# Causal mask by VectorE in the row minimum instead of by a matmul, in an attention and feed-forward kernel

## What is computed

```python
q = apply_rotary(pos, proj(Wq, bq) * scale)
k = apply_rotary(pos, proj(Wk, bk))
sim = jnp.einsum('bhid,bhjd->bhij', q, k)
causal = jnp.triu(jnp.ones((n, n), dtype=bool), k=1)
sim = jnp.where(causal, -jnp.finfo(sim.dtype).max, sim)
attn = jax.nn.softmax(sim, axis=-1)
out = jnp.einsum('bhij,bhjd->bhid', attn, v)
```

## Time and profile before

| what | us |
|---|---|
| median of three runs | 1103.43 |
| the three runs | 1103.32, 1103.43, 1105.03 |
| span of the profiled execution, first to last instruction | 1100.9 |
| TensorE matmuls busy | 1053.1 |
| VectorE busy | 807.6 |
| ScalarE busy | 672.6 |
| GpSimd busy | 615.8 |

### The profile page before, as it was taken

One profiled execution on the slowest core, in us unless ns is written; L12 is line 12 of the kernel. 1 busy time (PEld: TensorE's weight loads), 2 busy tenths in 40 slices (PEclk: granted clock), 3 DMA queues, 4 the chain that ended last, 5 costly groups with the idle time before them and its releaser, 6 DMA issues.

```text
span 1100.9 us, 20576 instructions
## 1 busy us (share of the span) xinstructions
PE 1053.1 (96%) x6624; PEld 917.1 (83%) x6624; DVE 807.6 (73%) x1451; ACT 672.6 (61%) x1443; POOL 615.8 (56%) x474
## 2 busy tenths in 40 slices
PE   6889999999999999999999999999999999988798
PEld 5778888888888888888888888888888888877676
DVE  6767877677767777787777776777677777769765
ACT  5466666566656666666566666666666666655642
POOL 3155655565556656565656555565566555674643
PEclk9899999999999999999999999999999999999999
DMA  9212211221112211211122111211122111320001
GB/s 282 68 36 61 49 30 40 68 48 38 31 31 68 48 39 40 67 44 34 31 68 48 39 39 31 68 39 39 40 67 49 39 37 31 107 78 1 11 29 39
DMA packets 41707, 56.60 MB, mean 51 GB/s; under 512 B 5204, under 2 KB 24724, under 8 KB 41620
## 3 DMA queue, kind: packets, MB, share of 16 engines
q1 hardware_dynamic: 41620, 55.30, 19.5%
HBM read 19.63 MB, written 2.10 MB: 20 GB/s over the span
## 4 chain that ended last, share of the span: by engine, by line
PE 76%; DVE 8%; POOL 6%; issue 5%; DMA 3%; ACT 2%; SPq 1%; DVEq 0%; ACTq 0%; POOLq 0%
PE ps_r L1179 14%; PE ps_r L1181 14%; PE ps_r L1180 14%; PE ps_t L1304 9%; PE ps_s L1179 5%; PE ps_s L1181 5%; PE ps_s L1180 5%; DMA swapped<-straight 2%; POOL swapped L566 2%; POOL straight L567 2%; PE ps_s L1186 2%; PE ps_s L1189 2%; POOL w_lo L559 1%; DVE v_lo L963 1%; PE ps_s L1289 1%
## 5 line engine op out<-in xcount | busy, mean ns | idle before, releaser
L566 POOL TENSOR_TENSOR swapped<-swapped,sin_sb 128x512 f32<-128x512 f32 x124 | 164.2, 1325 | 269.9 <-DMA swapped<-straight 269.7
L765 ACT ACTIVATE pT_hi<-ps_t 128x512 fp32r<-128x512 f32 (+3 forms) x384 | 187.8, 490 | 114.5 <-PE ps_t L1304 110.0
L1031 DVE TENSOR_TENSOR pT_lo<-ps_t,pT_hi 128x512 fp32r<-128x512 f32 (+3 forms) x384 | 204.1, 549 | 60.4 <-ACT pT_hi L765 55.0
L1055 DVE TENSOR_REDUCE neg_max<-ps_s 128x1 f32<-128x128 f32 (+7 forms) x256 | 192.1, 751 | 59.8 <-PE ps_s L1289 59.3
L573 POOL TENSOR_TENSOR qk_lo<-straight,qk_hi 128x512 fp32r<-128x512 f32 x124 | 158.8, 1290 | 130.5 <-ACT qk_hi L689 130.5
L776 ACT ACTIVATE probs<-ps_s,neg_max 128x128 f32<-128x128 f32 (+7 forms) x256 | 190.0, 742 | 23.8 <-DVE neg_max L1055 22.8
L1304 PE MATMUL ps_t<-ident,probs 128*128 128x128 f32 x1152 | 185.3, 274 | 7.5 <-DVE pT_lo L1031 7.4
L567 POOL TENSOR_TENSOR straight<-straight,cos_sb 128x512 f32<-128x512 f32 x124 | 178.8, 1442 | 0.0
L957 DVE TENSOR_TENSOR straight<-straight,swapped 128x512 f32<-128x512 f32 x126 | 133.8, 1062 | 27.9 <-POOL straight L567 27.6
L1179 PE MATMUL ps_s<-qk_hi 128*128 128x512 f32 (+3 forms) x384 | 141.9, 370 | 0.4 <-ACT probs L776 0.4
L1047 DVE SCALAR_TENSOR_TENSOR y<-ps_r,inv_sum,y 128x256 f32<-128x256 f32 x256 | 111.8, 478 | 34.0 <-PE ps_r L1181 29.5
(11 more groups left out here) (181 smaller groups left out, 2334.7 us busy)
## 6 DMA issues: line engine op xcount, KB each, us to landing
swapped<-straight SPq DMA_DIRECT2D x252, 128.0 KB, 2.3
x_in<-in_L_attn_x SPq DMA_DIRECT2D x4, 512.0 KB, 5.3
w_raw<-in_L_attn_Wk SPq DMA_DIRECT2D x8, 256.0 KB, 3.7
w_raw<-in_L_attn_Wq SPq DMA_DIRECT2D x8, 256.0 KB, 3.9
w_raw<-in_L_attn_Wv SPq DMA_DIRECT2D x8, 256.0 KB, 3.3
wo_all<-in_L_attn_Wo SPq DMA_DIRECT2D x1, 2048.0 KB, 11.5
wo_raw<-in_L_attn_Wo SPq DMA_DIRECT2D x8, 256.0 KB, 2.7
x<-in_L_attn_x SPq DMA_DIRECT2D x4, 512.0 KB, 4.1
```

The source lines that it names most:

```text
L566: pool.tensor_tensor(swapped[:, q, :], swapped[:, q, :], sin_sb[:, cs], ALU.mult)
L765: nc.scalar.activation(turned_at(ORDER[step], k0, k1)(pT_hi), ps_t[:, (T_FIRST[step] + j) % 2, 0:(k1 - k0) * P].rearrange("p (k q) -> p k ...
L1031: nc.vector.tensor_tensor(turned_at(t, k0, k1)(pT_lo), ps_t[:, (T_FIRST[step] + j) % 2, 0:(k1 - k0) * P].rearrange("p (k q) -> p k q", q=P ...
L1055: nc.vector.tensor_reduce(neg_max[:, t:t + 1], ps_s[:, step % 2, 0:(t + 1) * P], AX, ALU.max, negate=True).then_inc(max_ready, 1)
```

## The change

The mask matmul goes, and with it the bf16 identity and the 128 x 128 mask. A mask of 1024 columns, zero but for its last 128, takes their place. VectorE's reduction becomes one `tensor_tensor_reduce`: it adds the mask, multiplies by -1, writes the result back over the scores in PSUM and gives the row's minimum, which is the negated maximum. A nop ahead of it carries its wait. The exponential gets the scale -1. `attn_bias` moves into y[:, 0] to free its room.

```diff
-        ident_b = small("ident_b", [P, P], BF16)
-        mask_b = small("mask_b", [P, P], BF16)
-        attn_bias = small("attn_bias", [P, DIM], F32)
+        mask_wide = small("mask_wide", [P, SEQ], BF16)
...
-            pool.memset(mask_b[:, :], 0.0).then_inc(pool_chain, 1)
+            pool.memset(mask_wide[:, :], 0.0).then_inc(pool_chain, 1)
             pool.wait_ge(pool_chain, 2)
             pool.affine_select(out=ident[:, :], in_=ident[:, :], compare_op=ALU.not_equal, fill=1.0, base=0,
-                               pattern=[[-1, P]], channel_multiplier=1).then_inc(pool_chain, 1)
-
-            pool.affine_select(out=mask_b[:, :], in_=mask_b[:, :], compare_op=ALU.is_ge, fill=MASKED, base=0,
                                pattern=[[-1, P]], channel_multiplier=1).then_inc(consts_ready, 1)
-            pool.wait_ge(pool_chain, 3)
-            pool.tensor_copy(ident_b[:, :], ident[:, :]).then_inc(consts_ready, 1)
+
+            pool.affine_select(out=mask_wide[:, SEQ - P:SEQ], in_=mask_wide[:, SEQ - P:SEQ], compare_op=ALU.is_ge,
+                               fill=MASKED, base=0, pattern=[[-1, P]], channel_multiplier=1).then_inc(mask_ready, 1)
...
                 nc.scalar.activation(probs[:, P_AT[step] * P:(P_AT[step] + t + 1) * P], ps_s[:, step % 2, 0:(t + 1) * P],
-                                     ACT.Exp, bias=neg_max[:, t:t + 1],
+                                     ACT.Exp, bias=neg_max[:, t:t + 1], scale=-1.0,
                                      accum_out=row_sum[:, u % 2, t:t + 1]).then_inc(exp_ready, 1)
...
-            nc.vector.tensor_tensor(attn_bias[:, :], ps_s[:, 0, CH:CH + DIM], bo_wide[:, :], ALU.add)\
+            nc.vector.tensor_tensor(y[:, 0, :], ps_s[:, 0, CH:CH + DIM], bo_wide[:, :], ALU.add)\
                 .then_inc(attn_bias_ready, 1)
...
-            nc.vector.tensor_copy(y[:, :, :], attn_bias[:, None, :].broadcast_to([P, NTT, DIM])).then_inc(y_added, 1)
+            nc.vector.tensor_copy(y[:, 1:NTT, :], y[:, 0, None, :].broadcast_to([P, NTT - 1, DIM])).then_inc(y_added, 1)
+            dve.wait_ge(mask_ready, 1)
...
                 dve.wait_ge(scores_ready, ps.tiles(u, step + 1))
-                nc.vector.tensor_reduce(neg_max[:, t:t + 1], ps_s[:, step % 2, 0:(t + 1) * P], AX, ALU.max,
-                                        negate=True).then_inc(max_ready, 1)
+                dve.nop(nofuse=True)
+                n_keys = (t + 1) * P
+                rows = ps_s[:, step % 2, 0:n_keys]
+                nc.vector.tensor_tensor_reduce(rows, rows, mask_wide[:, SEQ - n_keys:SEQ], -1.0, -MASKED, ALU.add, ALU.min,
+                                               accum_out=neg_max[:, t:t + 1]).then_inc(max_ready, 1)
...
-                    diagonal = k0 + size == (t + 1) * P
-                    three(ps_s[:, step % 2, k0:k0 + size], q, qk_at(u % 2, 1, k0, size), True, not diagonal)
-
-                ins = nc.tensor.matmul(ps_s[:, step % 2, t * P:t * P + P], ident_b[:, :], mask_b[:, :],
-                                       start=False, stop=True)
+                    ins = three(ps_s[:, step % 2, k0:k0 + size], q, qk_at(u % 2, 1, k0, size), True, True)
                 ins.then_inc(scores_ready, 1)
...
-            pe.wait_ge(consts_ready, 2)
+            pe.wait_ge(consts_ready, 1)
```

More of the change, by code:

```diff
@@ L317, in build @@
         consts_ready = sem("consts_ready")
+        mask_ready = sem("mask_ready")
         c_ready = sem("c_ready")
@@ L605, in residual @@
                     .then_inc(pool_chain, 1)
-                pool.wait_ge(pool_chain, 4 + n)
+                pool.wait_ge(pool_chain, 3 + n)
                 pool.tensor_tensor(x2[part], x2[part], y[part], ALU.add).then_inc(x2_ready, 1)
```

## The result

The changed kernel takes 1076.03 us (median of four runs, 1073.16 to 1077.07) where the kernel before took 1103.61 in the same comparison (1103.32 to 1105.03). The ratio is 0.9741, with a 95% interval of 0.9722 to 0.9760: 27.6 us, where 16.4 were forecast. It lies outside the forecast range, on the fast side. The profiled execution took 1076.11 us, its span is 1074.3 us, 26.6 less than before.

The account below looks back on a forecast made before the run. TensorE was taken as the bound, never waiting in a dense unit. 21.1 us removed less 5.2 given back is 15.9, rounded up to 16.4: 1103.4 - 16.4 = 1087.0 us, range 1080.5 to 1099.

Parts of the forecast that it names:

- whatever leaves its queue shortens the unit: TensorE never waits in the 28.96 us dense attention unit, so removed work shortens it unless another engine becomes late.
- 192 slots: Mask matmuls standing between scores and transposes, 6 of 8 tiles a unit: 0.07 us saved each, 13.4 us.
- 64 slots with a surcharge: Mask matmuls ahead of a float32r matmul, which then holds longer: 0.12 us saved each, 7.7 us.
- the removal: Taking all 256 mask matmuls off TensorE: 21.1 us saved, rounded half a microsecond up.
- v_lo: TensorE's waits for v_lo lengthen as it arrives 0.33 us sooner: 16 x 0.27 = 4.3 us given back.
- VectorE's price: New combined operation against the plain reduction: 8 ns more; with its accumulator read 0.1 us per tile.
- The accumulator read: The new operation's minimum leaves VectorE through an accumulator: 0.09 us of queue time, ends 0 and 0.20.
- The last unit and the end: VectorE sets the pace there: five tiles save nothing (0.4 us) and each adds 0.1 us (0.5 us).
- VectorE takes over: Rival: the new operation runs at half rate per column, VectorE becomes the bound, 1126 us; chance 0.13.
- its formula: Rival's unit time: VectorE's work, 27.2 us, plus 2.45 us idle that stays, 29.7 us.
- Half of the gain lost: Rival: new operation has a fixed price of 0.3 to 0.4 us, or only bare slots go; about 1095 us; chance 0.18.
- no change: Rival: the v_lo wait spreads to every unit and takes the whole 0.66 us gained; 1103 us; chance 0.06.

Follow-up runs that it names:

- two part kernels: Kernel before with TensorE's part only (mask matmul left out, no masking), 1073.43 us; with VectorE's part only (new operation, mask of zeros, matmul kept), 1106.15 us.
- TensorE's part alone: Kernel before with the mask matmul left out and nothing in its place, VectorE keeping its reduction: 1073.43 us, ratio 0.9739.
- stepped kernels: Kernel before without the mask matmul in one step of four (1631 records a turn), 1104.43 us; in two of four (1615), medians 1093.33 and 1097.15 us.
- the dose of 256 columns: Changed kernel with an unneeded VectorE maximum over 256 columns behind each of the 256 new operations: 1078.55 us.
- the dosed kernel: Changed kernel with an unneeded VectorE maximum over 768 columns behind each of the 256 new operations: 1125.53 us, ratio 1.0186.

## Why the prediction was wrong

**The step that failed** is the one that priced only what stands inside a unit: "whatever leaves its queue shortens the unit", and then 192 slots and 64 slots with a surcharge as the whole of the removal. It put the loop's edge at nothing without a reason. The edge was never read, though the list of TensorE's waits named issue six times there (the "issue 5%" of the chain in the earlier trace rows alone would not have told: it is still 4% after). Removing instructions also shortened TensorE's program, its loop stopped being fetched in each turn, and 9.3 us of pauses went. The two part kernels show that this goes with TensorE's part alone, and the stepped kernels show that it comes at a point: all pauses at 1631 recorded instructions a turn, none or one at 1615. It isn't a price per instruction. Of the 11.2 us by which the forecast was short, the pauses are 9.3; the rest is that the removal was 1.5 us larger and less was given back for v_lo.

Of this, the Trainium skill (Runtime: NRT & Kernel Launch, Instruction fetch mechanics) says that a taken branch whose target lies outside the fetched window forces a fetch before execution goes on, and it gives TensorE 128 KiB for instructions. The pauses agree with the rule. The nine 16 KB packets of a turn of the kernel before are 144 KB, one packet more than 128 KiB holds; the loop itself is less than that (1647 records at some 250 a packet are 6.6 packets), and the ninth packet comes about 2 us ahead of the branch back. The page also says that prefetch is purely sequential with no cache, and puts the window at two pages; the changed kernel, with no packet of q8 for six turns, shows that a loop of over six packets can be kept.

**The removal** was forecast at 21.6 us and measured 23 (0.72 x 32): mechanism and both prices held, and the unit of 28.24 us lies in the 28.2 to 28.4 that the prediction named as its sign. Over the whole trace, the time from a mask's start to the next start was 0.066 us in the median ahead of transposes, and 0.039 us ahead of a float32r matmul, which then held 0.08 us more than its like. These add to 0.63 us a unit, a little under the 0.72.

**VectorE's price** was right: 8 ns forecast over the reduction and 7 to 9 measured. The accumulator read is a record of 139 ns, but the next operation starts with it, 0.60 us after the main operation's start (586.05 to 586.65 at 512 columns). Behind the plain reduction of the kernel before the next operation started after as long, 0.60 us in the median against 0.61 now. So the read takes none of the queue, and the 0.09 us that the prediction gave it were too much. That the new operation with its nop costs nearly nothing inside the loop is seen in the dose of 256 columns too.

**v_lo**: 4.3 us forecast as given back, 3.0 by gaps and about as much by units. The sign, the place and the mechanism were right: the gap grows by 0.4 us where 0.33 was forecast, and it does so with TensorE's part alone. The count was too high, since by starts there are eight gaps and not sixteen. The reason for the wait was half right: the prediction followed the chain back to GpSimd and called it the engine that sets it, where one swap in VectorE's own order removes the wait.

**The last unit and the end**: 0.9 us forecast. TensorE's waits for pT_lo in the last unit went from 4.7 to 5.6 us (5.2 with TensorE's part alone), and from the last exponential to the end it took 119.4 us in place of 117.8. But that end stretch differs by 2.9 us among the kernels of this study, whose code there is nearly the same, so nothing hangs on its 1.6. The ledger on spans: 23.0 + 9.3 - 3.0 for slots, pauses and v_lo, +0.8 for a first exponential that comes earlier, -1.6 for the end, is 28.5 against 26.6 measured. Of the missing 1.9, some are in the last unit, where the full 0.72 us is counted and the waits grew by 0.9; the rest is open.

**The rivals.** That VectorE takes over did not happen, and its formula was sound: in the dosed kernel it gives 30.0 us for a unit that takes 29.9. That this kernel also lands at 1125.5 us, where the rival was priced at 1126, is luck: the rival had a unit of 29.7 us, 0.2 to 0.3 less in each of 32, and kept the 9.3 us of pauses, which are gone here. Half of the gain lost and no change are excluded by the unit of 28.24 us. What was missing is a rival on the fast side: the range stopped at the reading error of the slots, as if nothing outside the units could improve.

## What to carry to other kernels

In a kernel with loops, read the waits named issue at the back edge and the packets on each engine's instruction queue before pricing an edit: an engine whose loop is fetched in each turn can gain a microsecond or more per turn from a few instructions fewer, all at once, and one whose loop just stays can lose as much from a few more. An edit that moves work to an engine with room costs little up to that engine's idle time less what it must wait for others (here 2.5 us in all for 45 us of extra work in the loop); that sum can be worked out from one unit, and in the one kernel that went past it here it held to 0.1 us. And before a wait is put down to a slow engine upstream, look at what stands just ahead of the late operation in its own queue.

## What the runs showed of the hardware

- TensorE's loop is either kept or fetched whole: 9 packets of 16 KB and a pause of 1.4 to 2.2 us in every turn at 1647 and 1631 recorded instructions; none at 1615 and 1583, but at 1615 once in six turns of one execution, with a pause of 2.5 us. Whether the count or the place of the packet borders sets the limit was not tested.
- Each engine's loop is kept or fetched by itself. VectorE's loop went from 266 to 330 recorded instructions and from no fetch to five packets of 8 KB a turn; it then stands about 2 us at each back edge (11.2 us in all), and since TensorE doesn't wait for it there, it costs little.
- An elementwise addition with a row minimum that reads PSUM and bf16 from SBUF and writes back into PSUM runs at the rate of a plain reduction: 683 against 676 ns at 512 columns. Its accumulator read takes none of the queue: the next operation starts 0.61 us after it, against 0.60 after the reduction.
- Seven stops of TensorE of up to 3.7 us each came with a granted clock at the lower level, 1.2 GHz, for 3.4 to 6.8 us (254.5 to 261.4 us in the kernel with GpSimd's order changed); 25.6 us of waits together, the kernel was 37 us slower. One stop of 1.7 us did so too, where pauses of up to 2.2 us in the same execution did not.
